# First layer of a two-layer cross-attention kernel: the work of a tile in a new order on every engine, statistics' DMAs on ScalarE's queue, preparation by thirds

## The reference

```python
a = _layer_norm(audio_kv, ln_gamma, ln_beta)                # 8 x 1500 x 256
Q = (hidden_states @ Wq.T).reshape(B, Tt, HEADS, HEAD_DIM)  # 16 heads of 16
K = (a @ Wk.T).reshape(B, Ta, HEADS, HEAD_DIM)
V = (a @ Wv.T).reshape(B, Ta, HEADS, HEAD_DIM)
scores = jnp.einsum('bhtd,bhsd->bhts', Q, K) * scale
attn = jax.nn.softmax(jnp.where(mask, scores, -inf), axis=-1)
out = jnp.einsum('bhts,bhsd->bhtd', attn, V) @ Wo.T
return hidden_states + jnp.tanh(gate) * out
```

## Time and profile before

| | |
|---|---|
| Median of three runs | 1966.26 us (1960.67 to 1976.54) |
| Profiled execution, its own time | 1976.77 us |
| Its span, first to last instruction | 1975.0 us |
| Mean granted TensorE clock | 0.949 |
| TensorE busy | 1739.3 us, 88% |
| VectorE / ScalarE / GpSimd busy | 1257.6 / 1023.0 / 482.0 us |
| First layer's preparation / its 64 tiles | 104 us / 441 us |

### The profile page before, as it was taken

The page is one execution under the profiler, slowest core; times in us unless marked ns, Lnnn a source line. Parts: engine busy times, 40 slices in busy tenths (PEclk is TensorE's granted clock), DMA queues, the critical chain, the costliest instruction groups (busy, mean ns, idle before and its releaser), DMA issues.

```text
span 1975.0 us, 32767 instructions
## 1 busy us (share of the span) xinstructions
PE 1739.3 (88%) x9974; PEld 1486.3 (75%) x9974; DVE 1257.6 (64%) x2513; ACT 1023.0 (52%) x1857; POOL 482.0 (24%) x334
## 2 busy tenths in 40 slices
PE   2388888888759999999999998699999999999986
PEld 2377777777647888888888886578888888888875
DVE  3376666676567666666656657776666666666574
ACT  2265666575435555555555546355555455555462
POOL 4264454552134011011101103440110011011042
PEclk7799999999779999999999998899999999999988
DMA  6645667654224011001001102240110011010021
GB/s 188 157 125 148 163 164 179 154 137 119 63 64 145 9 60 62 31 31 62 32 31 62 62 1 67 77 138 19 45 62 31 31 62 48 15 62 0 1 67 52
DMA packets 113905, 149.50 MB, mean 76 GB/s; under 512 B 25433, under 2 KB 99681, under 8 KB 113833
## 3 DMA queue, kind: packets, MB, share of 16 engines
q1 hardware_dynamic: 113832, 148.61, 27.2%
HBM read 108.28 MB, written 3.42 MB: 57 GB/s over the span
## 4 chain that ended last, share of the span: by engine, by line
PE 63%; issue 7%; DVE 4%; POOL 2%; ACT 2%; DVEq 0%; PEld 0%; POOLq 0%; PEldq 0%; ACTq 0%
PE ps L893 16%; PE ps L662 10%; PE ps L664 10%; PE ps L663 10%; PE ps L895 8%; PE ps L863 7%; PE ps L874 1%; POOL cx L631 1%; PE ps L762 0%; DVE rr L1540 0%; POOL khl L503 0%; DVE o_row L1562 0%; ACT o_low L1232 0%; PE ps L968 0%; POOL raw_t L514 0%
## 5 line engine op out<-in xcount | busy, mean ns | idle before, releaser
L893 PE MATMUL ps<-cx,rr 128*128 128x512 f32 x1344 | 484.6, 403 | 15.8 <-DVE rr L1540 14.0
L1216 ACT ACTIVATE rr<-ps 128x512 fp32r<-128x512 f32 x336 | 198.7, 597 | 349.7 <-PE ps L863 349.7
L895 PE MATMUL ps<-cx,rr 128*128 128x256 f32 x1344 | 374.8, 279 | 0.0
L893 PEld LDWEIGHTS ps<-cx,rr 128*128 128x128 f32 x1344 | 252.4, 188 | 74.6 <-issue 19.4
L662 PE MATMUL ps<-ct,rr 128*128 128x500 f32 x672 | 280.7, 418 | 6.6 <-ACT ar L1200 6.6
L1540 DVE TENSOR_TENSOR rr<-ps,rr 128x512 fp32r<-128x512 f32 x336 | 231.4, 690 | 55.5 <-ACT rr L1216 40.0
L664 PE MATMUL ps<-ct,rr 128*128 128x500 f32 x672 | 261.7, 389 | 0.0
L663 PE MATMUL ps<-ct,rr 128*128 128x500 f32 x672 | 260.7, 388 | 0.0
L895 PEld LDWEIGHTS ps<-cx,rr 128*128 128x128 f32 x1344 | 253.9, 189 | 0.0
L1562 DVE SCALAR_TENSOR_TENSOR o_row<-ps,rinv,o_low 128x256 f32<-128x256 f32 x112 | 54.1, 483 | 309.9 <-ACT o_low L1232 309.9
L1514 DVE TENSOR_REDUCE mx<-ps 128x1 f32<-128x500 f32 x336 | 226.8, 676 | 11.7 <-PE ps L664 3.5
(11 more groups left out here) (183 smaller groups left out, 3221.8 us busy)
## 6 DMA issues: line engine op xcount, KB each, us to landing
raw_t<-in_ctx_t SPq DMA_DIRECT2D x24, 1500.0 KB, 6.4
k<-khl SPq DMA_DIRECT2D x192, 187.5 KB
raw<-in_ctx SPq DMA_DIRECT2D x24, 1408.0 KB
raw<-stat_scratch SPq DMA_DIRECT2D x8, 750.0 KB, 4.0
ar<-in_wq SPq DMA_DIRECT2D x32, 128.0 KB, 3.5
ar<-in_wk SPq DMA_DIRECT2D x32, 128.0 KB, 3.6
ar<-in_wv SPq DMA_DIRECT2D x32, 128.0 KB, 2.2
ar<-in_wo SPq DMA_DIRECT2D x32, 128.0 KB, 2.1
```

Source lines behind the costliest of these rows:

```text
L893: pe.matmul(ps[:, 6, :], pt[0:n, 0, c, :], cx[0:n, c, :], start=c == 0, stop=False, skip_group_check=True)
L895: mm = pe.matmul(ps[:, 6, 0:D], pt[0:n, 1, c, :], cx[0:n, c, 0:D], start=False, stop=c == CH - 1, skip_group_check=True)
L1216: act.activation(pt[:, 0, GRP * k:GRP * (k + 1), :], ps[:, 3 + k, :].rearrange("p (c q) -> p c q", q=P), ACT.Copy)\
```

## The change

Six things change, in the first layer only.

- A slot's order. TensorE: scores of g+1, third group of turns of tile g-1 (before: of tile g, at the end), `keys`, weighted sum of g-1, groups 0 and 1 of g, `values`. ScalarE: high part of group 2 of g-1, copy of the last slot's `values`, copy of `keys`, exponential of g+1, `output`, high parts 0 and 1. VectorE: `row_max`, low part of group 2 of g-1, low part of the last slot's `values`, reciprocals, `bn_stats`, `collapse`, low parts 0 and 1.
- `spread` is two products of 224 columns into bank 6, with `sel` as weights and a smaller `ra`. GpSimd makes `ra` at t = 2, TensorE reads it at t = 4, ScalarE copies at t = 5, GpSimd's `normalise` is at t = 6.
- The store and the broadcast of the statistics are issued by ScalarE: the store right behind the copy to `mv_row`, the broadcast by `spread_stats` one slot later, behind the copy of `keys`.
- Preparation: `bn_stats` of batch 0 comes before the first low parts, that of batch 1 before the scaling of batch 0; the broadcast of batch 0 goes into a buffer of its own (`rs_first`), raw of batch 1 is loaded as soon as `bn_stats` is done, raw_t of batch 0 is scaled by thirds (two by VectorE, one by GpSimd), `keys` goes by halves of heads (`K_FIRST`), `values` comes before the first scores.
- SyncE begins the first four `stack`s when the first half of `keys` is done.
- The mask is handled on 96 partitions.

```diff
@@ constants, buffers
+K_FIRST = [(0, 0), (0, 1), (0, 2), (1, 0), (1, 1), (1, 2)]
+MC = 12
-            ra = zb("ra", [QR, 4, P])
-            sel = zb("sel", [QR, P])
+            ra = zb("ra", [QR, 2, 4, TQ])
+            sel = zb("sel", [QR, 2, P])
+        rs_first = o_c_flat[:, 0:S]
@@ sync
-            token_stats(0)
-
+            sp.wait_ge(s["bn_done"], 1)
+            load_raw(0, 1)
...
-            sp.wait_ge(s["at_p"], 1)
-            sp.wait_ge(s["at_v"], 1)
-            load_raw(0, 1)
-            sp.wait_ge(s["zcl"], 2)
-            sp.wait_ge(s["zcv"], 1)
+            sp.wait_ge(s["zcl"], 1)
+            sp.wait_ge(s["zcv"], 2)
             load_raw_t(0, 1)
             sp.wait_ge(s["mk_out"], 16)
             sp.wait_ge(s["q3_out"], 16 * 3 * PAIRS)
+            sp.wait_ge(s["zkl"], 2)
+            sp.wait_ge(s["zkv"], 1)
+            for p in range(HPB):
+                stack(0, p, True)
             sp.wait_ge(s["zkl"], 3)
             sp.wait_ge(s["zkv"], 3)
-            for p in range(PAIRS):
+            for p in range(HPB, PAIRS):
                 stack(0, p, True)
-            token_stats(1)
...
                 load_raw_t(0, b + 2)
-                token_stats(b + 2)
                 wait_apart(sp, s["zkl"], 6 * b + 8)
@@ gpsimd, slot
-                if t == 0 and not zero(b):
+                if t == 2 and not zero(b):
                     spread(b - 1, 1 - n)
-                if t == 1 and not zero(b):
-                    normalise(b - 1)
...
+                if t == 6 and not zero(b):
+                    normalise(b - 1)
@@ gpsimd, preparation
+            variance(0)
             for n, dst in enumerate((wk_s, wv_s)):
...
-            variance(0)
-            scale(0, 0)
-            ct_low(0, 0)
+            v = slice(2 * SB, S)
...
+            pool.tensor_tensor(raw_t[:, :, v], raw_t[:, :, v], rs_first[:, v].rearrange("p (o t) -> p o t", o=1)
+                               .to_broadcast([P, DH, SB]), ALU.mult).then_inc(s["at_p"], 1)
             ct_low(0, 2)
+            variance(1)
@@ tensor
-            def spread(b, bank, col):
+            def spread(b, bank):
                 pe.wait_ge(s["zra"], b + 1)
-                for g in range(4):
-                    mm = pe.matmul(ps[:, bank, col + TQ * g:col + TQ * (g + 1)], ra[:, g, :], bsel[:, :], start=True,
-                                   stop=True)
+                for a in (0, 1):
+                    mm = pe.matmul(ps[:, bank, 0:4 * TQ], sel[:, a, :], ra[:, a, :, :].rearrange("k g q -> k (g q)"),
+                                   start=a == 0, stop=a == 1)
...
-                    weighted(b if t else b - 1, (t - 1) % SLOTS, g - 1, n if t else 1 - n, bank_free)
-                transposes(g, t, 0)
-                transposes(g, t, 1)
+                    transposes(g - 1, (t - 1) % SLOTS, 2)
                 if t in K_AT and kind != "plain":
                     u = K_N[t]
                     pe.wait_ge(s["zks"], 6 * (b + 1) + u)
                     keys(b + 1, u, *K_AT[t], 5)
+                if t or later:
+                    if t == 4 and kind == "full":
+                        pe.wait_ge(s["stat_row"], b + 3)
+                    weighted(b if t else b - 1, (t - 1) % SLOTS, g - 1, n if t else 1 - n)
+                transposes(g, t, 0)
+                transposes(g, t, 1)
                 if t == 3 and kind == "full":
                     pe.wait_ge(s["zoc"], g)
                     turn_stats(b + 2)
-                transposes(g, t, 2)
@@ scalar
                 act.activation(mv_row[:, :], ps[0:CH, 7, 256:256 + P], ACT.Copy).then_inc(s["stat_row"], 1)
+                wait_apart(act, s["stat_row"], b + 1)
+                act.dma_start(st_d, mv_row[:, :]).then_inc(s["stat_out"], 16)
+
+            def spread_stats(b):
+
+                wait_apart(act, s["stat_out"], 16 * (b + 1))
+                dst = rs_first if zero(b) else rs_b
+                act.dma_start(dst, st_d.rearrange("c p -> (c p)")[0:S].partition_broadcast(P)).then_inc(s["stat_in"], 16)
...
+            def high_probs(g, k):
+                act.wait_ge(s["ztr"], 3 * g + k + 1)
+                high(pt0[:, GRP * k:GRP * (k + 1), 0:QR],
+                     ps[:, 3 + k % 2, 0:GRP * QR].rearrange("p (c q) -> p c q", q=QR)).then_inc(s["zph"], 1)
...
+                if kind == "full" and t == 4:
+                    spread_stats(b + 2)
...
+                if t or later:
+                    output(g - 1)
+                high_probs(g, 0)
+                high_probs(g, 1)
                 if kind == "full":
                     if t == 3:
                         turn_stats(b + 2)
                     if t == 6:
                         ct_high(b + 2, 0)
+                        ct_high(b + 2, 1)
@@ vector
+            load_stats(0, 0, CH)
             dve.wait_ge(s["x_hi"], 1)
...
+            load_stats(1, 0, CH)
             dve.wait_ge(s["b0_sum"], 1)
...
+                if t or later:
+                    low_probs(g - 1, 2)
+                if u_last is not None and (t or later) and not (kind == "plain" and t):
+                    values(b + 1 if t else b, u_last, 1 - n if t else n, 6)
+                if t == 0 and later:
+                    reciprocals(b - 1, 1 - n)
+                if kind == "full" and t in (1, 2):
+                    load_stats(b + 2, 6 * (t - 1), 6 * t)
...
                 if t or later:
                     collapse(b if t else b - 1, (t - 1) % SLOTS, g - 1)
                 low_probs(g, 0)
                 low_probs(g, 1)
```

More of the change, by code:

```diff
@@ L561, in slot @@
                         scale(b + 2, t - 4)
+                if t == 6 and not zero(b):
+                    normalise(b - 1)
+                if kind == "full":
                     if t == 6:
@@ L797, in slot @@
                     pe.wait_ge(s["zvl"], 6 * (b + 1) + u)
+                    if t == 6 and later:
+                        pe.wait_ge(s["zre"], b)
                     values(b + 1, u, 6)
-                if t == 0 and later:
-                    pe.wait_ge(s["zoc"], g)
-                    spread(b - 1, 7, 256)
+                if t == 4 and later:
+                    if kind != "plain":
+                        pe.wait_ge(s["zvl"], 6 * (b + 1) + 4)
+                    spread(b - 1, 6)
                 if kind == "plain" and t == SLOTS - 1:
                     pe.wait_ge(s["zks"], 6 * B)
-                    spread(b, 5, 0)
+                    spread(b, 5)
             pe.wait_ge(s["w0_lo"], 3)
@@ L821, in _ @@
             whole_batches(pe, slot, "full", "keys", "plain")
-            weighted(B - 1, SLOTS - 1, GT0 - 1, 1, lambda: None)
+            transposes(GT0 - 1, SLOTS - 1, 2)
+            weighted(B - 1, SLOTS - 1, GT0 - 1, 1)
             pe.wait_ge(s["wo_hi"], 1)
@@ L1089, in slot @@
                 later = not zero(b)
+                u_last = V_AT.get((t - 1) % SLOTS)
                 if t or later:
-                    output(g - 1)
-                for k in (0, 1):
-                    act.wait_ge(s["ztr"], 3 * g + k + 1)
-                    high(pt0[:, GRP * k:GRP * (k + 1), 0:QR], ps[:, 3 + k, 0:GRP * QR].rearrange("p (c q) -> p c q", q=QR))\
-                        .then_inc(s["zph"], 1)
+                    high_probs(g - 1, 2)
+                if u_last is not None and (t or later) and not (kind == "plain" and t):
+                    if u_last == 0 and later:
+                        act.wait_ge(s["zpv"], SLOTS * b)
+                    values(b + 1 if t else b, u_last, 1 - n if t else n, 6)
+                if t in K_AT and kind != "plain":
+                    u = K_N[t]
+                    act.wait_ge(s["zkl"], 6 * (b + 1) + u - 4)
+                    keys(b + 1, u, 5)
+                if kind == "full" and t == 4:
+                    spread_stats(b + 2)
                 if not (kind == "plain" and t == SLOTS - 1):
@@ L1108, in slot @@
                         ct_high(b + 2, 0)
+                        ct_high(b + 2, 1)
                     if t == 7:
                         ct_high(b + 2, 2)
-                act.wait_ge(s["ztr"], 3 * g + 3)
-                high(pt0[:, 2 * GRP:3 * GRP, 0:QR], ps[:, 3, 0:GRP * QR].rearrange("p (c q) -> p c q", q=QR))\
-                    .then_inc(s["zph"], 1)
-                if t in V_AT and kind != "plain":
-                    u = V_AT[t]
-                    if u == 0 and later:
-                        act.wait_ge(s["zpv"], g)
-                    values(b + 1, u, 1 - n, 6)
-                if kind == "full" and t == 6:
-                    ct_high(b + 2, 1)
-                if t == 0 and later:
-                    spread(b - 1, 7, 256)
+                if t == 5 and later:
+                    spread(b - 1, 6)
                 if kind == "plain" and t == 3:
@@ L1445, in slot @@
                 later = not zero(b)
+                u_last = V_AT.get((t - 1) % SLOTS)
                 if not (kind == "plain" and t == SLOTS - 1):
                     row_max((t + 1) % SLOTS, g + 1)
```

(10 more changed lines are left out.)

137 lines of the change are left out of this document (58 added, 79 removed).

## The result

The changed kernel took 1908.2 us, median of 4 runs (1903.22 to 1910.21), and the kernel before, on the same chip, 1971.4 (4 runs). The ratio is 0.968, 95% interval 0.962 to 0.974: faster by about 63 us. The forecast was 1902.

The account below looks back on a forecast made before the run. The prediction took TensorE as the bound, with holes that are waits for other engines. Preparation 26 us, seven batches 36 and the end 3 sum to 65 us, from the median of 1,966.26 to 1,902 us, range 1,880 to 1,925.

Parts of the forecast that it names:

- Preparation, first half: Batch 0's statistics and scaling by thirds on two engines: first `keys` product near 38 us, 5.5 us earlier.
- Preparation, second half: Batch 1's statistics: store at 50, first `keys` product at 67.5, 32.6 us earlier; 5 to 6 given back for raw.
- A batch: Eight tiles of the first layer: 51 us (48 to 56) against 56.2, over seven batches 36 us gained.
- The ring: Chain in each tile from `row_max` through exponential and copies to the next `row_max`: 5.4 us, below which no tile goes.
- There the 32.4 us go: TensorE's 32.4 us of waits for VectorE's low copies ahead of transposes vanish, as third transposes move one tile later.
- The slow clock behind `spread`: Clock of 0.50 right behind a stall at `spread`, each batch; that stall goes, 0.7 us a batch kept for others.
- Tile 7: ScalarE comes late from two `ct_high` copies, the weighted sum waits 2.4 us, and the tile takes 6.8 us.
- ScalarE's DMAs: Two statistics DMAs a batch issued by ScalarE cost 0.7 us a batch (bounds 0 and 4).
- The rival by the clock: Slower, 1,990 us: batches of 63.8 us, a share of 0.49 of each at 1.2 GHz; chance 0.05.
- The holes: Rival: holes in the batches refill as raw comes late and DMA is full, 4 us a batch lost; 1,935 us, chance 0.18.
- the queue's rival: ScalarE's queue gives little: broadcast waits among the stacks, the preparation gains only 5 us; 1,922 us, chance 0.07.
- more: Rival with a larger gain: batches at 48 us and no slow clock; 1,878 us, chance 0.10.

Follow-up runs that it names:

- the edits above: New kernel with another order of the keys, raw of batch 2 loaded earlier, four `bn_stats` a tile and GpSimd's third behind VectorE's two: 1892.93 us, ratio 0.961.
- the other kernel: New kernel, but in the preparation GpSimd multiplies its third of raw_t only when VectorE has done its two: 1907.26 us, ratio 0.967.

## Why the prediction was right

The three terms came out at 26.1, 37.7 and 2.9 us where 26, 36 and 3 were forecast (the last as a net of two parts), 66.6 for 65. The sign held, and the time lay in the range. The terms match better than their steps do. The forecast's 26 us already had the wait for raw of batch 2 in them (5 to 6 us); the measured 26.1 has not, since the wait stands behind tile 1. Put where the forecast had it, its 5.1 us make the preparation 21.0 us for 26, and the tiles 42.8 for 36: two errors of 5 and 7 us that cancel, and luck in the agreement by terms. The steps, one by one:

- **Preparation, first half: right, by two errors that cancel.** The scaling began at 32.9, not 34; VectorE's two thirds then took 4.4 us, not 2.6. The first product came at 38.53 for 38.
- **Preparation, second half: right.** Store at 51.2 for 50; scaling at 60.4, between the 57 and 63 given; batch 1's first product at 70.7 between 67.5 and 73, so 29.5 us earlier for 32.6; 4.2 us of wait for raw for 5 to 6, at a cost of 5.1. Not counted was that tile 1's exponential now stands behind the copy of the first keys, 3.4 us. With the DMAs back on SyncE's queue 21 of the 26 us are gone. The Trainium skill (DMA: Bandwidth & Descriptors, Issuing engines are not separate DMA queues) says that a second queue saves the issuing time alone, "which is usually small relative to the DMA itself". The transfer did slow among the stacks (6.6 us from issue to scaling for 4.1 before), and one issue is small here too, 0.2 to 0.9 us; but 40 of them stood ahead in SyncE's order, and that place was worth 21 us.
- **A batch: right, 50.8 for 51, in part by luck.** The forecast used 51 for all seven. A batch that prepares another takes 50.0 to 50.2 us at full clock and 52.0 to 52.5 with a slow stretch; the first has 5.1 us of wait for raw in its 54.7, and batch 6, which takes no statistics, needs 46.2. The surplus of the one and the lack of the other (some 4 to 5 us each) nearly cancel. Tile 3 took 8.86 us for 9.1, with the wait for low 0 at 1.27 for 2.3 and that for `collapse` at 0.86 for 0.7. The short tiles stand 5.6 and 5.3 apart for 5.4; 7 to 9 us apart are two exponentials in each full batch (7.4 to 8.2), not one. The ring was not the floor that was claimed: in the last batch tiles follow each other at 5.18 us.
- **"There the 32.4 us go": wrong.** Only 14.7 of them went, and the same wait for low copies ahead of the weighted sum grew by 15.8: in one-step tiles the low copy of group 2 is late by up to 1.4 us, which the sum of the ring had not shown as a wait. What went is TensorE's 16.9 us ahead of `spread` and the waits ahead of the scores. Of the 44 us that the window is shorter, 24 are busy time of TensorE and 20 idle time. From start to start a `keys` product takes 0.42 us at the lower clock and 0.23 at the higher, 1.8 times; by that some 28 of the 62 us were lost to the clock before and 11 of the 24 now. These are estimates; they put 17 of the 24 us of busy time down to the clock, and 3.7 are `spread`'s cheaper products (9.0 us for 12.7). The forecast said 0.7 us a batch for the new kernel, 4.9 in all, where 13.7 us at the lower clock in the seven batches cost some 6, and it never counted the old one's; it came out right since it worked forward from instruction times at full clock.
- **The slow clock behind `spread`: borne out.** In the kernel before it follows each of the six stalls of more than 2 us, 34 of the 43 us at 1.2 GHz from 104 to 494; stalls of 0.7 us had none behind them. It is not `spread`'s alone: with waits ahead of transposes (2.1 us each in the mean) the mean clock fell to 0.87 without a stall at `spread`. Of the stalls that were to bring it back, those of tile 3 have no slow stretch behind them, and that of tile 7 is 1.2 us, not 2.4. The stretches of 3.4 us in batches 1 and 3 of the new kernel stand behind a wait of 1.35 us in tile 6 (at 168.1 and 270.3), which other batches have without a fall.
- **Tile 7: wrong.** It was to take 6.8 us for two `ct_high`; they run for 1.96 us at 273.02 and cost nothing, since the exponential behind them waits for the scores: 5.91 us, or 7.5 where the clock is low.
- **ScalarE's DMAs: 0.7 us a batch was too much.** The issues take 0.32 and 0.35 us, and full batches at full clock take 50.2 us with them and 50.5 to 50.6 with the DMAs on SyncE's queue, so no cost shows.

The rival by the clock did not come, but slower was possible: the third group in its own tile made 2035.55 us, with a clock of 0.87 and more lost to waits than to the clock. The rival's sum has a slip: 1.6 times compares durations of products that overlap, and from start to start it is 1.8, so a share of 0.36 of a batch at 1.2 GHz would have been enough for its pace of 63.8, not 0.49. The holes and the queue's rival did not come; "more" comes only with the edits above.

## What to carry to other kernels

Where TensorE is the bound with holes, ask how long each wait is as well as what they sum to, above all for a wait that comes in every tile: with pieces of 0.7 and 1.3 us in the mean the clock was 0.97, with pieces of 2.1 us it was 0.87, and the slow clock then added an estimated 44 us to the 62 of the waits. Moving a group of work one step later, so that its wait is over when the engine comes to it, is the part of this change that it could least do without: taken back, it cost 127 us. And when one wait is taken away, look in the queue of the next engine for an operation that stands behind somebody else's wait: with one `bn_stats` in place of six, TensorE's wait for GpSimd's power (9.7 us) took back all that VectorE gave, and fell to 1.4 us only when the order of the keys let the power through.

## What the runs showed of the hardware

**VectorE stands still beside GpSimd.** A multiplication of VectorE (128x1000) with both inputs in SBUF that begins 1.08 us after GpSimd's takes 3.29 us for 1.15, and ends 1.06 us after GpSimd's end. The second low part did the same in the other kernel. The profile books the wait as busy time of VectorE. GpSimd seems to wait as well: its multiplication takes 3.31 and 3.20 us, both times begun while one of VectorE's was under way, and its subtraction of the same shape takes 2.36 with VectorE clear of it:

```profile
39.35 2.36 POOL L499 TENSOR_TENSOR ct<-raw_t,ct 128x1000 fp32r<-128x1000 f32 x1 [1.15 <-ACT ct L1026]
```

No run has GpSimd's multiplication alone. The Trainium skill (SBUF — State Buffer, Who interferes with whom) says that such an operation contends with a GpSimd one that reads SBUF, and that the one that issued first blocks the other for the whole instruction: the traces agree.

**A stall that no wait explains.** In both kernels with one `bn_stats`, and in no other, VectorE's timeline has a hole in front of the first instruction behind the loop's branch back, `row_max` in tile 1 of batch 3 (batches 1 and 2, then 3 and 4 are the loop's two rounds):

```profile
242.05 1.72 DVE L1434 TENSOR_REDUCE neg<-ps 112x1 f32<-112x1500 f32 x1 [13.16 <-issue]
```

The scores had long been there, and in the new kernel the exponential behind this `row_max` comes 5.95 us after the one before it, here 18.5. The DMA view of the same kernel, 224 to 245 in 40 slices, has the engines full until some 2 us before the hole ends (228.9 to 242.05), and two queues that carry code:

```profile
DMA  9899999989999899999777999999982210000000
...
q8 instruction: 1, 0.02, 0.4%
q14 instruction: 3, 0.02, 0.3%
```

The Trainium skill (Runtime: NRT & Kernel Launch, Instruction fetch mechanics) says that a branch to code outside the loaded pages makes the engine wait for a fetch by DMA. That fits the place, the branch, and the full DMA engines. It is not shown that these packets were VectorE's: the new kernel has three on the same two queues between 215 and 245, and no hole. No run settled it; why the branch costs nothing in the kernels with all twelve `bn_stats` stays open.
